# A ViT layer on one core: GpSimd sums part of the patches of x by folding additions

## The reference

```python
# tokens: sums over 16 x 16 patches, then a mix of the 12 channels
pooled = x.reshape(64, 12, 14, 16, 14, 16).sum(axis=(3, 5))
h = einsum('bcij,ce->bije', pooled, channel_weights)      # (64, 196, 192)
# attention over the 196 tokens of an image, 12 heads, polynomial instead of a softmax
q, k, v = split(layernorm(h) @ w_qkv)
a = relu(1 + qk + qk**2 / 2); a = a / a.sum(-1)
h = h + (a @ v) @ w_proj + b_proj
# mixture of experts: router with 8 experts, top 2, each 192 -> 768 -> 192 with gelu
h = h + sum_e weight_e * (gelu(layernorm(h) @ w1[e] + b1[e]) @ w2[e] + b2[e])
```

## Time and profile before

| | |
|---|---|
| median of three runs | 1360.76 us (1356.45 to 1372.45) |
| span of the profiled execution, first to last instruction | 1353.8 us |
| mean granted TensorE clock | 0.937 |
| busy: TensorE, VectorE, ScalarE, GpSimd | 91%, 71%, 44%, 44% |
| VectorE's 448 reductions of x | 359.2 us |

### The profile page before, as it was taken

How to read it: one execution, slowest core, us unless ns; L and a number is a source line. 1 busy time by engine, 2 the same in 40 slices (tenths; PEclk the granted TensorE clock), 3 DMA queues, 4 the chain that set the end, 5 groups by cost and what they waited for, 6 DMA issues and landing times.

```text
span 1353.8 us, 26903 instructions
## 1 busy us (share of the span) xinstructions
PE 1228.0 (91%) x7299; PEld 1093.9 (81%) x7299; DVE 956.8 (71%) x3407; ACT 596.2 (44%) x1127; POOL 600.4 (44%) x483
## 2 busy tenths in 40 slices
PE   5867766999999999899999899999999979999997
PEld 3756655888888888788888788888888879998996
DVE  6799998787878787877787687868783523333454
ACT  1221223454545454445444354535454534544664
POOL 0104333425454454453644545464555464533433
PEclk9986556999999999898999899989999989999999
DMA  9679887767878887778786878877744655544555
GB/s 354 231 254 347 320 281 262 231 220 240 238 232 221 255 216 245 204 238 218 234 246 217 210 237 234 250 208 234 195 129 80 211 117 130 107 95 89 119 142 112
DMA packets 126551, 284.42 MB, mean 210 GB/s; under 512 B 24819, under 2 KB 70500, under 8 KB 126500
## 3 DMA queue, kind: packets, MB, share of 16 engines
q1 hardware_dynamic: 82762, 241.95, 54.5%
q0 software_dynamic: 43104, 41.25, 17.7%
q10 hardware_dynamic: 634, 0.61, 0.2%
HBM read 228.79 MB, written 54.95 MB: 210 GB/s over the span
## 4 chain that ended last, share of the span: by engine, by line
PE 33%; DMA 19%; DVE 17%; POOL 15%; issue 14%; ACT 1%; POOLq 1%; SPq 0%; ACTq 0%; DVEq 0%
PE ps L993 11%; DMA result<-ys,ridx 11%; PE ps L962 10%; POOL rows_d L608 8%; DMA rows_d<-rows,sloti 7%; POOL result L623 7%; DVE red L1069 6%; PE ps L802 3%; PE ps L933 2%; PE ps L934 2%; DMA w1r<-L_attn_w_qkv 1%; DVE stats L1197 1%; DVE topi L1206 1%; PE ps L1022 1%; DMA xr<-rows_d 1%
## 5 line engine op out<-in xcount | busy, mean ns | idle before, releaser
L623 POOL DMA_INDIRECT result<-ys,ridx x210 | 333.1, 1586 | 307.9 <-issue 120.4
L993 PE MATMUL ps<-w2a,hid 128*128 x2520 | 455.5, 327 | 0.0
L608 POOL DMA_INDIRECT rows_d<-rows,sloti x256 | 258.9, 1011 | 394.0 <-DMA rows_d<-rows,sloti 146.7
L993 PEld LDWEIGHTS ps<-w2a,hid 128*128 128x128 f32 x2520 | 415.4, 190 | 11.8 <-issue 0.2
L1069 DVE TENSOR_REDUCE red<-xbuf 128x21 f32<-128x672 f32 x448 | 359.2, 841 | 5.3 <-PE ps L866 2.4
L727 ACT ACTIVATE hid<-ps,b1s 128x512 f32<-128x512 f32 (+1 forms) x344 | 222.9, 654 | 239.2 <-PE ps L962 230.5
L962 PE MATMUL ps<-xh,w1h 128*128 128x512 f32 (+1 forms) x344 | 166.0, 482 | 7.9 <-DVE xl L1306 3.9
L1329 DVE TENSOR_TENSOR w1l<-w1r,w1h 128x768 fp32r<-128x768 f32 x116 | 110.3, 951 | 70.9 <-ACT w1h L739 70.3
L962 PE MATMUL ps<-xh,w1l 128*128 128x512 f32 (+1 forms) x344 | 131.5, 382 | 0.0
L962 PE MATMUL ps<-xb,w1h 128*128 128x512 f32 (+1 forms) x344 | 131.3, 382 | 0.0
L962 PE MATMUL ps<-xl,w1h 128*128 128x512 f32 (+1 forms) x344 | 131.2, 381 | 0.0
(11 more groups left out here) (164 smaller groups left out, 1633.8 us busy)
## 6 DMA issues: line engine op xcount, KB each, us to landing
xbuf<-x SPq DMA_DIRECT2D x224, 672.0 KB, 5.6
w1r<-L_ffn_w SPq DMA_DIRECT2D x118, 384.0 KB, 3.7
xr<-rows_d SPq DMA_DIRECT2D x48, 402.0 KB, 3.4
result<-h1s SPq DMA_DIRECT2D x32, 294.0 KB
w2a<-L_ffn_w SPq DMA_DIRECT2D x8, 576.0 KB, 7.6
rows_d<-rows,sloti POOLq DMA_INDIRECT x256
rows_d<-pad SPq DMA_DIRECT2D x9, 402.0 KB, 4.6
result<-ys,ridx POOLq DMA_INDIRECT x210, 4.9
```

The costliest lines, as they stand in the source:

```text
L608: pool.indirect_dma_start(rows_d, bass.IndirectOffsetOnAxis(ap=sloti[:, k * NT + t:k * NT + t + 1], axis=0), rows[:, t, :], None).then_inc ...
L623: pool.indirect_dma_start(out, bass.IndirectOffsetOnAxis(ap=ridx[:, b, n:n + 1], axis=0), ys[:, b, n, :], None, compute_op=ALU.add).then_i ...
L993: last = mm(yout(g, b, n), hid[:, m % 3, cols], w, start=False, stop=m == MC - 1 and n % 2 == 1)
```

## The change

GpSimd sums 23 of the chunks of steps -1 to 3 in VectorE's place. It has five dependent additions for a chunk: columns 0 to 15 plus 16 to 31, in place, then 8, 4, 2, and the last pair into `red`. Which chunks: 2, 5, 8 and 11 in the setup (P(-1)); 1, 3, 5, 7, 9, 11 and 13 in P(0), behind the setup's and ahead of the padding additions; in each of the lone steps 0, 1 and 2 the chunks 4 and 6 ahead of the wait at t = 3, and 9 and 11 ahead of the wait at t = 6, which are the next step's share P(s + 1). VectorE skips them, and draws forward seven of the P that are left to it in step 0. Who waits for sums (SyncE's loads, S1) waits for both engines' counters.

```diff
@@ -176,6 +176,11 @@
 ]
 PARTS = CHUNKS * HALVES
 LOW_BY_DVE = (0, 1, 2)
+POOL_FIRST = (2, 5, 8, 11)
+POOL_SECOND = (1, 3, 5, 7, 9, 11, 13)
+POOL_ALONE = ((4, 6), (9, 11), ())
+POOL_LONE = sum(POOL_ALONE, ())
+FOLDS = EIGHTH.bit_length() - 1
 assert STEP_ALONE.count("P") == sum(o.count("P") for o in ORDER) == LAST.count("P") == PARTS
 
 
@@ -332,7 +337,7 @@
         s_dvs = sem("dve_setup")
         s_dvp = sem("dve_pick")
         s_dvg = sem("dve_gate")
-        s_pooled = sem("pooled")
+        s_pooled, s_pooled2, s_fold = sem("pooled_by_dve"), sem("pooled_by_pool"), sem("folded_by_pool")
         s_mix = sem("mix_ready")
         s_phi = sem("phi_ready")
         s_g, s_phT = sem("moments_ready"), sem("phiT_turned")
@@ -390,6 +395,31 @@
 
             return ps[0:NF, 3 + h % FB, 0:4 * NF].rearrange("p (a b f) -> p b a f", a=2, b=2)
 
+        early = [True]
+
+        def by_pool(s):
+
+            if isinstance(s, int) and s < 1:
+                return POOL_SECOND if s == 0 else POOL_FIRST
+            return POOL_LONE if early[0] else ()
+
+        def chunks_to(s, k):
+
+            known = isinstance(s, int) and s < 1
+            each = 0 if known or not early[0] else len(POOL_LONE)
+            here = sum(q <= k for q in by_pool(s))
+            done = (0, len(POOL_FIRST))[s + 1] if known else                 len(POOL_FIRST) + len(POOL_SECOND) + (-each if each else (PRO - 1) * len(POOL_LONE))
+            return (CHUNKS - each, CHUNKS + k + 1 - done - here), (each, done + here)
+
+        def wait_pooled(eng, s, k):
+
+            (a, b), (c, d) = chunks_to(s, k)
+            eng.wait_ge(s_pooled, s * (HALVES * a) + HALVES * b)
+            if c:
+                eng.wait_ge(s_pooled2, s * c + d)
+            elif d:
+                eng.wait_ge(s_pooled2, d)
+
         now = [0, -1]
 
         def loads_to(ahead, each):
@@ -404,6 +434,7 @@
 
             part = 0
             lone[0] = not with_tiles and not last
+            early[0] = not with_tiles
             rank_bank[0] = 6 if lone[0] else 2
             lists = [LAST if last else STEP_ALONE]
             if with_tiles:
@@ -474,7 +505,7 @@
             for k in range(XSLOTS):
                 load_chunk(0, k)
             for k in range(CHUNKS):
-                sp.wait_ge(s_pooled, HALVES * (k + 1))
+                wait_pooled(sp, -1, k)
                 load_chunk((k + XSLOTS) // CHUNKS, (k + XSLOTS) % CHUNKS)
 
 
@@ -490,7 +521,7 @@
             def P(s, p):
                 k = p // HALVES + XSLOTS
                 if p % HALVES == HALVES - 1 and (k < CHUNKS or steps_left[0]):
-                    sp.wait_ge(s_pooled, s * PARTS + PARTS + p + 1)
+                    wait_pooled(sp, s, p // HALVES)
                     load_chunk(s + 1 + k // CHUNKS, k % CHUNKS)
 
             def load_rows(j, buf, listed, first=False):
@@ -592,6 +623,32 @@
             nc.gpsimd.memset(cwT[:, :, 0:1], 0.0)
             nc.gpsimd.memset(b2t[:], 0.0)
             given("pool", "fills", nc.gpsimd.memset(rstd1[:], 1.0))
+
+            def P(s, k):
+
+                each, to = chunks_to(s, k)[1]
+                folds = s * (each * (FOLDS - 1)) + (to - 1) * (FOLDS - 1)
+                wait_first(pool, d_x[k % XSLOTS],
+                           (s + 1) * (16 * CHUNKS // XSLOTS) + 16 * (k // XSLOTS) + 16)
+                v = xbuf[:, k % XSLOTS].rearrange("p h n w -> p (h n) w")
+                for f in range(FOLDS):
+                    w = EIGHTH >> (f + 1)
+                    if f < FOLDS - 1:
+                        nc.gpsimd.tensor_tensor(v[:, :, 0:w], v[:, :, 0:w], v[:, :, w:2 * w], ALU.add).then_inc(s_fold, 1)
+                        wait_first(pool, s_fold, folds + f + 1)
+                    else:
+                        nc.gpsimd.tensor_tensor(red[:, k * HALVES * SUMS:(k + 1) * HALVES * SUMS].unsqueeze(2),
+                                                v[:, :, 0:w], v[:, :, w:2 * w], ALU.add).then_inc(s_pooled2, 1)
+
+            def P_group(s, group):
+
+                if group:
+                    wait_first(pool, s_mix, s + 1)
+                for k in group:
+                    P(s, k)
+
+            for k in POOL_FIRST[:1]:
+                P(-1, k)
             pool.wait_ge(d_w, 16 * 9)
             set_wait(pool, "pool", "zeros")
             given("pool", "pad", nc.gpsimd.tensor_copy(pad[:, :, ROW - 1:ROW].bitcast(I32), padi[:].unsqueeze(2)))
@@ -603,11 +660,15 @@
                     wait_first(pool, s_slots, s + 1)
                 for t in (2 * q, 2 * q + 1):
                     if t in (3, 6):
+                        if lone[0]:
+                            P_group(s + 1, POOL_ALONE[t // 6])
                         wait_first(pool, d_scat, s * (32 * NT) + t * 32)
                     for k in range(2):
                         pool.indirect_dma_start(
                             rows_d, bass.IndirectOffsetOnAxis(ap=sloti[:, k * NT + t:k * NT + t + 1], axis=0),
                             rows[:, t, :], None).then_inc(d_scat, 16)
+                if q == 3 and lone[0]:
+                    P_group(s + 1, POOL_ALONE[2])
 
             def F(j, b):
 
@@ -640,6 +701,9 @@
                 nc.gpsimd.tensor_tensor(w1l[:, :, cols], w1r[:, nb, q], w1h[:, :, cols].bitcast(F32),
                                         ALU.subtract).then_inc(s_w1l, 1)
 
+            for k in POOL_FIRST[1:]:
+                P(-1, k)
+            P_group(0, POOL_SECOND)
             wait_first(pool, d_pad, 32)
             for n in range(TP):
                 pool.indirect_dma_start(
@@ -859,7 +923,7 @@
 
             def S1(s):
 
-                pe.wait_ge(s_pooled, s * PARTS + PARTS)
+                wait_pooled(pe, s - 1, CHUNKS - 1)
                 for hf in range(2):
                     for g in range(GROUPS):
                         o = g * NTOK + hf * TOK
@@ -1062,6 +1126,8 @@
             def P(s, p, first=False):
 
                 k, h = p // HALVES, p % HALVES
+                if k in by_pool(s):
+                    return
                 if p == 0 and not first:
                     dve.wait_ge(s_mix, s + 1)
                 if h == 0:
@@ -1072,6 +1138,7 @@
 
             n_set = [0]
             n_early = [0]
+            ahead_of_loop = [p for p in range(PARTS) if p // HALVES not in POOL_SECOND][:7]
 
             def link(ins):
 
@@ -1079,7 +1146,7 @@
                 ins.then_inc(s_dvs, 1)
                 dve.wait_ge(s_dvs, n_set[0])
 
-            pooled = iter(range(PARTS))
+            pooled = iter([p for p in range(PARTS) if p // HALVES not in POOL_FIRST])
 
             def pool_first(n):
 
@@ -1362,15 +1429,15 @@
                 out=amat[:], in0=ps[0:U, 6, 0:HEADS * U].rearrange("p (h u) -> p h u", h=HEADS), scalar=HD ** -0.5,
                 in1=const("e00", U).unsqueeze(1).to_broadcast([U, HEADS, U]), op0=ALU.mult, op1=ALU.add))
             set_wait(dve, "pool", "fills")
-            pool_first(PARTS - 12)
+            pool_first(PARTS - HALVES * len(POOL_FIRST) - 12)
             for _ in range(2):
-                P(0, n_early[0])
+                P(0, ahead_of_loop[n_early[0]])
                 n_early[0] += 1
             S2(0)
             for h in range(HEADS):
                 if h in (2, 4, 6, 8, 10):
                     for _ in range(1):
-                        P(0, n_early[0])
+                        P(0, ahead_of_loop[n_early[0]])
                         n_early[0] += 1
                 set_wait(dve, "act", f"factors{h}")
                 if h:
@@ -1381,7 +1448,7 @@
             given("dve", "score", V.tensor_scalar(score[0:1, :, 0:1], score[0:1, :, 0:1], 0.5, None, ALU.add))
 
             def P_left(s, p):
-                if after_first(s) or p >= n_early[0]:
+                if after_first(s) or p not in ahead_of_loop:
                     P(s, p)
 
             schedule(dve, {"P": P_left, "S1": S1, "S2": S2, "T2": T2, "S6": S6, "S7": S7, "S8": S8, "S10": S10, "R": R,
```

## The result

The changed kernel takes 1423.05 us, median of four runs (1404.98 to 1425.93); the kernel before, beside it, 1362.45. The ratio is 1.042, 95% interval 1.034 to 1.050: slower, above the range of the prediction. The profiled execution took 1423.59 us (span 1421.8), 68.0 us over the span of before.

A forecast was written before the change was run, and what follows sets the result against it. VectorE looked like the lone steps' bound, with TensorE's low-clock chain next; TensorE bound the later part. Setup -1.3, lone periods +2.6 and step 3 +2.2 gave +3.5 us on 1360.76: forecast 1364.3, range 1355 to 1380.

The forecast's parts named there:

- The small things: Second semaphore for each consumer and the waits' own increments: said to lie beside work, with no time booked.
- if the difference arises behind S1 of step 4: Sign that the forecast is wrong: time changing in the later part, which the change was said to leave alone.
- From S1 of step 4 on, TensorE is the bound: Later steps: TensorE bounds them, so a shift arriving there is passed on whole.
- Rival 1: Setup: GpSimd's folds hold back VectorE's two-input instructions in S2(0), 10 us more, 1374 in all; chance 0.3.
- predicted 1.3: Setup and step 0: VectorE's shortened block of reductions gains 1.3 us, TensorE's chain being next.
- The fold: GpSimd's five dependent additions for one chunk: taken as 3.75 us, range 3.0 to 4.8.
- VectorE's relief is worth little because TensorE's chain is next: Lone step: VectorE loses 6.7 us of work, worth about 1.4 us of time.
- Lone steps, GpSimd's side: Folds end at T+29.8, making S1 and landed scatters late: +1.3 us for each of two periods, +2.6 together.
- the first tile behind it: Step 3: step 2's delayed scatters hold the first tile's load 4.0 us; after slack and omitted reductions, +2.2 us.
- rival 2: Slower folds, 4.8 us a chunk: lone periods and step 3 grow further, +16 us, 1377 in all; chance 0.12.
- the prediction's own rule: Lone steps: each 0.1 us more for a chunk's fold adds 0.4 us to a period.

The follow-up runs named there:

- e13: Kernel before, loop in its old place, with 14 further always-satisfied SyncE waits a step in one place; chip D: 1358.1 us, ratio 0.999.
- c3: Changed kernel, but in the main loop SyncE waits for VectorE's counter alone before loads of x; chip E: 1425.1 us, ratio 1.050.
- c1: Changed kernel, unaltered, run again on chip E: 1419.6 us, ratio 1.045 to the kernel before.
- e2: Kernel before, no folds, with 90 tiny VectorE memsets early in the setup that move its loop; chip A: 1370.4 us, ratio 1.010.
- c2: Kernel before, no folds, with 90 tiny VectorE memsets that move its loop; chip E: 1396.0 us, ratio 1.029.
- e6: Changed kernel with 38 VectorE memsets restoring the loop's place, step 0's folds started only after VectorE finished S2(0); chip A: 1371.8 us, ratio 1.011.
- e1: Changed kernel with 38 tiny VectorE memsets early in the setup, so its main loop lies where it did before; chip A: 1372.8 us, ratio 1.011.
- e5: Changed kernel with only the lone steps' twelve folds and 16 VectorE memsets keeping the loop's place; chip B: 1376.3 us, ratio 1.015.
- e4: Changed kernel with only the eleven folds of steps -1 and 0 and 22 VectorE memsets keeping the loop's place; chip B: 1360.0 us, ratio 1.002.
- e3: Changed kernel, but in the main loop SyncE waits for VectorE's counter alone before loads of x; chip A: 1387.2 us, ratio 1.021.
- e8: Changed kernel with 24 VectorE memsets, so its loop lies 14 instructions before its old place; chip C, one run: 1388.4 us.

## Why the prediction was wrong

- **The failed step** is "The small things (a second semaphore for each consumer, the waits' own increments) lie beside work", with the setting of the whole sum that the change leaves the part from 230 us on alone. Semaphores were indeed free (e13, c3 against c1). What was missing from the small things is that VectorE's program became shorter ahead of its loop. That moved the loop, and cost 12 us on one kind of chip, 39 on the other (e2, c2). The first trace of the changed kernel, 49.6 us longer in the ten passes, is of the costly kind. The prediction named this as what would make it wrong ("if the difference arises behind S1 of step 4"), but gave it no price and no chance. "From S1 of step 4 on, TensorE is the bound" held, and is why pauses of 4.6 us a pass on VectorE, on TensorE's path, counted.
- **Rival 1** came true in kind and was over-priced: S2(0) took 10.4 us instead of 4.9, 5.5 of the 10 booked, and e6 shows that 6 us of first scatter hang on it. As the reductions left out had won 3 (predicted 1.3), the net at the first scatter was +2.1. The Trainium skill (SBUF — State Buffer, Who interferes with whom) has the rule; the phi products above at 3.90 instead of 1.57 us and the reductions, unchanged at 842 ns, agree with it.
- **The fold** was taken as 3.75 us and is 4.31, inside 3.0 to 4.8. The Trainium skill's figure (GPSIMD Engine Reference, 3.1) had given, as an estimate, 2.9 us before starts and gaps; the five additions take 3.7.
- **VectorE's relief is worth little because TensorE's chain is next**: right, the reciprocal waits 2.44 us for the product.
- **Lone steps, GpSimd's side**: right in mechanism, mis-sized. Folds end at T+32.8, not T+29.8, of which the fold's price makes 4 x 0.56 = 2.2 us and the gaps before and in the scatters the rest. The two periods grew by 4.6 and 3.1 us in the profile instead of 1.3 each; the third, up to step 3's first scatter, by 7.1, where I had booked 2.2 for the first tile behind it (4.0 - 0.3 - 1.5, with a slack given as 0.4 just before). S11 of that period, too, waited for landings (3.85 us), which I had booked for the two full periods only. Sum of the three: 14.8 us in this profile, e1 over e2 on chip A 14.5 (46.5 + 46.0 + 43.4 against 41.8 + 43.1 + 36.5), against 4.8 predicted; e5 over e4 on chip B 11.4. That is rival 2's mechanism, near its size (+16), but at c = 4.31: by the prediction's own rule, 0.4 us for each 0.1 us of c, the price of the fold alone makes 2.2 us of a period, and rival 2 had taken 4.8.
- **Without the moved loop** the change is e1: 1372.8, slower by 1.1%, inside the range of 1355 to 1380, where rivals 1 and 2 had put it, not the forecast. The two parts add up nearly there: 11.7 (e2) and 14.0 (e1) of the 28.5 us of e3, which has both.

On chips of the costly kind the parts are 39 (c2) and 16.9 (e5 over before), 56 of 62.5 (c1 over before). The remaining 7 are within the intervals. But the changed kernel with its loop in the old place was not run on such a chip; the nearest, e8, is a single run and 10 us above e5's 17.

**Open.** Why three chips have late hand-overs, fetches or no fetches, is not explained: a copy 3.2 or 3.3 us after its matmuls is seen there, its cause isn't. Why the fetches cost three times as much there is explained in part only, by the low clock; and that the low clock follows from the gaps was read from the traces, not tried. The price of a place other than -38, -14, 0 and +90 instructions wasn't measured.

## What to carry to other kernels

Instructions added or taken away ahead of a loop move the loop's code; here this alone was worth 1 to 3%, as much as what the change was about, or more: look at the instruction queue's packets within the loop, before and after, ahead of any explanation by the work. Pad the program to undo the shift, and then judge the change. Compare kernels, and traces, only with those taken beside them on the same chip: a difference between two runs on different chips led me through several runs to a cause that did not exist. Look for a sign by which the traces tell the chips apart (here ScalarE's waits "<-remote"), and see whether it is there without the supposed cause too. And a fold is hidden by a wait only up to that wait's length: one chunk of 4.3 us in a 5.4 to 6.8 us wait left the step as long as it was, two made it longer.

## What the hardware showed unexpectedly

- A loop of VectorE, some 300 instructions a pass, runs without any fetch at two places measured (0, and 14 earlier in e8), and with five 8 KB fetches a pass at 38 earlier and at 90 later, two places 128 instructions apart. The pauses are 1.35 and 3.26 us. The Trainium skill (Runtime: NRT & Kernel Launch, Instruction fetch mechanics) says that a taken branch to a page outside the current two forces a fetch before the engine goes on, which fits the packet and the pause behind the jump back. It speaks of 16 KiB blocks, while the trace's packets carry 0.42 MB / 51 = 8 KB. The measurement decides for this chip.
- Two kinds of chip that agree within 0.3% on the kernel before (1357.0 to 1361.1) differ by 26 us on the same kernel with its loop moved (1370.4 and 1396.0). On one kind ScalarE starts some copies over 3 us after the matmuls that they wait for, in kernels with and without fetches (c2, e4).
- GpSimd's additions: 1.63 us for 672 elements a partition, 0.26 us for 42.
